# A planned one-core transformer loop: the causal mask moved from TensorE to VectorE, exponentials taken per head, gate columns carried by the value product, and the weight preparation moved into the loop

## What is computed

```python
# layer 0: self attention (causal), cross attention, feed-forward; 16 heads of 16
energy = where(cols >= length, -inf, Q @ K.T);  energy = where(cols > row, -inf, energy)   # causal: self only
z = softmax(energy / 4) @ V;  x1 = layernorm(x + z, ln1)
x2 = layernorm(x1 + mha(x1, ctx), ln2)
x3 = layernorm(x2 + relu(x2 @ fc1.T + b1) @ fc2.T + b2, ln3)
# layer 1 ("pair"): NX = layernorm(ctx, n1), NF = layernorm(x3, n2), one head of 256
h = gelu(softmax(NF @ NX.T / 16) @ NX @ gate.T + gate_b)      # 4 columns: the gates
cross = h @ w_cross.T + b;  NC = layernorm(cross, n3)
x4 = NF + gam2 * (cross + gam1 * softmax(NC @ NC.T / 16) @ NC)
# layer 2 ("real"): x5 = x4 + softmax(x4 @ ctx.T) @ ctx
# layer 3 ("mix"): 8 heads of 32; keys and values from layernorm(ctx, g1)
x6 = x5 + mha(layernorm(x5, g1), layernorm(ctx, g1));  U = (layernorm(x6, g2) @ W_in.T + b_in) @ Bmat
s = silu(s @ A.T) + U[t]                                       # a scan over the 128 rows
out = x6 + s @ Cmat + mean(program_probs) @ W_prog.T + b_prog
```

## Time and profile before

| | |
|---|---|
| median of 3 runs | 4208.76 us (4208.7 to 4211.23) |
| profiled execution, its time | 4207.95 us |
| its span | 4206.2 us |
| PE busy | 4042.6 us, 96% |
| weight loads of PE busy | 3383.5 us, 80% |
| DVE busy | 3431.2 us, 82% |
| ACT busy | 3175.7 us, 76% |
| POOL busy | 2911.0 us, 69% |

### The profile page before, as it was taken

The page is one execution under the profiler, slowest core; times in us unless marked ns, Lnnn a source line. Parts: engine busy times, 40 slices in busy tenths (PEclk is TensorE's granted clock), DMA queues, the critical chain, the costliest instruction groups (busy, mean ns, idle before and its releaser), DMA issues.

```text
span 4206.2 us, 112214 instructions
## 1 busy us (share of the span) xinstructions
PE 4042.6 (96%) x37547; PEld 3383.5 (80%) x37547; DVE 3431.2 (82%) x9517; ACT 3175.7 (76%) x6733; POOL 2911.0 (69%) x3172
## 2 busy tenths in 40 slices
PE   4899999999999999999999999999999999999859
PEld 3688888888888888888888888888888888888645
DVE  3688888888888888888888888888888888888634
ACT  1577887887788778877887787788778877887632
POOL 0477777777777777777777777777777777777634
PEclk9999999999999999999999999999999999999979
DMA  3000100010001100000100010101000000100037
GB/s 108 19 25 25 33 30 28 25 33 30 28 25 33 30 28 26 30 29 27 31 30 28 25 33 30 28 25 33 30 28 26 30 28 25 33 30 25 17 103 272
DMA packets 116547, 159.98 MB, mean 38 GB/s; under 512 B 11350, under 2 KB 103323, under 8 KB 111579
## 3 DMA queue, kind: packets, MB, share of 16 engines
q1 hardware_dynamic: 111626, 146.75, 11.2%
q10 hardware_dynamic: 4368, 6.17, 0.5%
HBM read 115.01 MB, written 37.88 MB: 36 GB/s over the span
## 4 chain that ended last, share of the span: by engine, by line
PE 67%; ACT 12%; POOL 7%; issue 5%; DVE 4%; DMA 0%; ACTq 0%; DVEq 0%; POOLq 0%; SPq 0%
PE bank L674 15%; PE bank L744 9%; PE bank L666 7%; PE bank L682 6%; PE bank L858 4%; PE bank L714 3%; ACT prob L992 3%; PE bank L778 3%; PE bank L693 3%; PE bank L773 2%; POOL rs_ln L1404 2%; PE bank L791 2%; POOL X L1424 2%; POOL X L1418 2%; ACT probT L1002 2%
## 5 line engine op out<-in xcount | busy, mean ns | idle before, releaser
L1158 DVE TENSOR_REDUCE mx<-bank 128x4 f32<-128x512 f32 x1280 | 837.6, 681 | 90.4 <-PE bank L714 68.6
L1169 DVE TENSOR_TENSOR prob<-bank,mx 128x512 f32<-128x512 f32 x1280 | 847.8, 679 | 54.6 <-PE bank L744 33.8
L1002 ACT ACTIVATE probT<-bank 128x512 f32<-128x512 f32 x1280 | 753.3, 600 | 158.9 <-PE bank L778 100.5
L992 ACT ACTIVATE prob<-prob 128x512 f32<-128x512 f32 x1280 | 795.6, 641 | 22.0 <-DVE prob L1169 20.9
L982 ACT ACTIVATE turned<-bank 128x512 f32<-128x512 f32 x896 | 531.9, 616 | 344.0 <-PE bank L666 223.5
L744 PE MATMUL bank<-ident,prob 128*128 128x128 f32 x5120 | 746.3, 277 | 20.3 <-DVE den L1180 6.5
L744 PEld LDWEIGHTS bank<-ident,prob 128*128 128x128 f32 x5120 | 591.3, 142 | 124.9 <-issue 36.8
L674 PE MATMUL bank<-turned,shared 128*128 128x256 f32 x2560 | 605.7, 384 | 1.8 <-ACT turned L982 1.8
L674 PEld LDWEIGHTS bank<-turned,shared 128*128 128x128 f32 x2560 | 468.3, 191 | 69.9 <-issue 14.3
L1404 POOL TENSOR_TENSOR rs_ln<-ve_ln,half 128x2 f32<-128x2 f32 x320 | 226.4, 707 | 384.9 <-DVE ve_ln L1147 384.9
L1483 POOL TENSOR_SCALAR shared<-turned,half_of 128x512 f32<-128x512 f32 x256 | 399.1, 1570 | 79.9 <-ACT turned L982 79.9
(11 more groups left out here) (242 smaller groups left out, 9047.8 us busy)
## 6 DMA issues: line engine op xcount, KB each, us to landing
shared<-in_x SPq DMA_DIRECT2D x128, 256.0 KB, 3.0
CB<-in_ctx SPq DMA_DIRECT2D x64, 256.0 KB, 3.4
CC<-in_ctx SPq DMA_DIRECT2D x64, 256.0 KB, 2.8
mod<-mod_rows SPq DMA_DIRECT2D x64, 256.0 KB, 3.3
residual<-X SPq DMA_DIRECT2D x64, 256.0 KB, 3.5
out<-turned SPq DMA_DIRECT2D x16, 1024.0 KB, 4.8
turned<-residual SPq DMA_DIRECT2D x14, 1024.0 KB, 7.3
u_turned<-us SPq DMA_DIRECT2D x64, 64.0 KB, 2.4
```

The lines of the kernel that those rows point to most:

```text
L992: nc.scalar.activation(flat(t), flat(t), ACT.Exp, scale=SCALE[p]).then_inc(*st["act"].mark(f"exp.{b}{r}"))
L1002: nc.scalar.activation(flat(t), banks.of(f"{att}.turn.{b}{r}")[:, :], ACT.Copy).then_inc(*st["act"].mark(f"probT.{b}{r}"))
L1158: nc.vector.tensor_reduce(m[:], banks.of(f"{att}.tile.{b}{r}")[:, :].rearrange("p (h t) -> p h t", h=4), AX, ALU.max)\
L1169: nc.vector.tensor_tensor(t[:], banks.of(f"{att}.tile.{b}{r}")[:, :].rearrange("p (h t) -> p h t", h=4), maxes.of(f"{att}.max.{b}{r}")[:]. ...
```

## The change

The self tiles lose `causal` on PE. DVE now adds the mask while it copies the bank into the `prob` buffer (`mask.br`), and takes the negated maximum out of that buffer (`max.br`); ACT takes the exponential in four instructions of 128 x 128, one a head, each with its head's negated maximum as bias; the scale 1/4 is folded into the query weights. The bank is free after `mask`, and the `prob` buffer is held from `mask` on.

The 4 gate columns ride on the value product of the mix layer (`w_v3`, 260 columns a batch, two banks, two `vp3` buffers). `vx`, its evacuation, `a4r`, `a4`, `yT` and its evacuation are gone. DVE divides the probabilities themselves (`part1`, two instructions of 128 x 128). `av1` has weights of 4 columns and moves 128, one batch in each of two strips, ACT takes the gelu of it with the bias column in two instructions of 4 x 128, and `cross` has weights of 32 rows, one batch in each strip and in a bank of its own, evacuated in two instructions. `mix_out.u` has weights of 64 columns, one batch in each half of the array.

The two blocks ahead of the loop are gone. Seven loads (identity, three weights of the first projections, three small ones) and the ordering of two weights stand ahead of it. The weights of the cross attention are loaded in turn 1, all others in turn 2 (54 DMAs in SP's queue), the probabilities in turn 2 from ACT's queue. The preparation (`prepare`) stands at the head of turn 3 on PE, ACT, DVE and POOL. The sum of the probabilities is now a tree of additions. `PROGRAM` and `BANKS` are written anew throughout; the number of turns is the same.

```diff
-                def causal_(b, r):
...
-                        nc.tensor.matmul(t[:, :], ident_b[:], causal[:].rearrange("p h t -> p (h t)"), start=True, stop=False,
-                                         skip_group_check=True).then_inc(*self_att["pe"].mark(f"causal.{b}{r}"))
...
-                                                    KEYS[p][rows_, a, :, b * S:(b + 1) * S], start=(p != "self"), stop=True,
-                                                    skip_group_check=(p == "self"))
+                                                    KEYS[p][rows_, a, :, b * S:(b + 1) * S], start=True, stop=True)
...
-                def vx(g):
...
+                def v3(g):
...
+                            last = nc.tensor.matmul(t[:, 0:D + 4], trn["HCT"][:, a, b * S:(b + 1) * S], w_v3[:, a, :],
+                                                    start=(a == 0), stop=(a == DH - 1))
...
-                        last = nc.tensor.matmul(t[:, b * 4:b * 4 + 4], pct["1"][:, b, :], vxs[:, b, :], start=True, stop=True)
+                        last = nc.tensor.matmul(t[32 * b:32 * b + 4, 0:S], vp3[g % 2][:, b, D:D + 4], pct["1"][:, b, :], start=True, stop=True)
...
-                def yT(g):
...
-                        last = nc.tensor.matmul(t[:, b * D:(b + 1) * D], y5T[:, b, :], w_cross[:], start=True, stop=True)
+                    for b, (t, _) in enumerate(took):
+                        rows_ = slice(32 * b, 32 * b + 32)
+                        last = nc.tensor.matmul(t[:, 0:D], y5T[rows_, :], w_cross[rows_, :], start=True, stop=True)
...
-                        last = nc.tensor.matmul(t[:, 0:W], w_u[:, a, :], trn["H6T"][:, a, :], start=(a == 0), stop=(a == DH - 1))
+                        for b in range(G):
+                            last = nc.tensor.matmul(t[NS * b:NS * b + NS, 0:S], w_u[:, a, :], trn["H6T"][:, a, b * S:(b + 1) * S],
+                                                    start=(a == 0), stop=(a == DH - 1))
...
+                def prepare():
...
+                    for w in latest(*(banks.free(n) for n in PREP_BANKS)):
+                        pe.wait_ge(*w)
+                    pe.wait_ge(rest_in, REST)
+                    pe.wait_ge(prep, 4)
+                    pe.wait_ge(ordered, 6)
...
+                    pe.wait_ge(prep, 8)
+                    pe.wait_ge(turned_b, 4)
+                    pe.wait_ge(means, 6)
...
+                    def masked(g):
...
+                        low = maxes.of(f"{att}.max.{b}{r}")
+                        for h in range(4):
+                            last = nc.scalar.activation(t[:, h, :], t[:, h, :], ACT.Exp, bias=low[:, h:h + 1], scale=1.0)
...
+                    def mask_(g):
+                        t, free = probs.claim(f"{att}.mask.{b}{r}", st["pe"], f"turn.{b}{r}")
...
+                        nc.vector.tensor_tensor(t[:], banks.of(f"{att}.tile.{b}{r}")[:, :].rearrange("p (h t) -> p h t", h=4),
+                                                causal[:].unsqueeze(1).to_broadcast([128, 4, 128]), ALU.add).then_inc(*st["dve"].mark(f"mask.{b}{r}"))
...
+                        nc.vector.tensor_reduce(m[:], probs.of(f"{att}.mask.{b}{r}")[:], AX, ALU.max, negate=True)\
...
+                def part1(g):
...
+                    for b in range(G):
+                        last = nc.vector.tensor_scalar(pc["1"][:, b, :], pc["1"][:, b, :], rsum["1"][:, b:b + 1], None, ALU.mult)
...
+def drive(eng, rings, handlers, engine, ahead=None):
...
+    for i in range(NG + LAGS):
+        if i in ahead:
+            ahead[i]()
         for unit, name, lag in ORDER[engine]:
```

712 lines of the change are left out of this document (354 added, 358 removed).

## The result

The changed kernel takes 4143.65 us (median of 4 runs, 4143.01 to 4149.18) beside 4208.73 for the kernel before in the same session: a ratio of 0.985, 95% interval 0.983 to 0.986. That is -65 us, where -227 was predicted; the time lies outside the range of 3900 to 4085. The profiled run took 4143.4 us.

What follows compares the result with a forecast made beforehand. TensorE's list was taken to bound the loop: its edits save 3.1 us a group, 62 x 3.1 = 192, and the start 35, so 4208 - 192 - 35 = 3981 us. Forecast 3945 to 4030 (0.50), wider range 3900 to 4085.

Steps and rivals of the forecast that it cites:

- What is taken from it shortens all 64 groups, as long as the others keep up.: Loop: TensorE's list, busy 60.5 of a 60.7 us turn, sets the turn, so cuts there shorten every group.
- 6.06 of 6.06 us: Profile reading of a loop stretch where ScalarE had nothing to spare; cited as a risk to hiding its added work.
- ScalarE's +4.2 us: Loop: four exponentials per self tile, 0.26 us each, for one of 0.52; +4.2 us a group, hidden on the average.
- Rivals 4 and 5: ScalarE half uncovered, 1.5 us a turn, 4074 us (0.06); slower, self exponentials' added time on the path, 4241 us (0.05).
- the sign I named: Forecast wrong if TensorE has over 1 us of new idle time a turn released by ScalarE's exponentials or evacuations.
- The narrow products: Loop, TensorE: `av1` -0.2, `cross` -0.4 and `u` -0.3 us a group from using narrow strips of the array.
- scores: Loop, TensorE: five bursts of three tiles and a lone tile cost +0.6 us a group, bounds +0.4 to +1.1.
- Rival 1: Narrow products gain nothing: -2.0 us a group, 4049 to 4085 us; changes of shape might add +0.8 a turn; chance 0.14.
- The bound of -3.9: Loop: largest saving a group on TensorE, with the bounds of its edits all on one side; the other end -1.7.
- VectorE no change, mask and maximum: Loop: mask addition and maximum out of the buffer cost VectorE the same for 8 tiles, within 0.05 us each.
- The start: Before the loop fills: first turn of x1 at 75 us in place of 110, -35 us, bounds -20 to -45.
- The end: Last turns and scan: number of turns, lags and scan taken as the same, so no change in time.

Runs made afterwards that it cites:

- e2: Changed kernel with ScalarE's two evacuations of `cross` moved ahead of the two `ln1` instructions; 4196.0 us.
- e5: Changed kernel with the gelu of the gates replaced by a copy with bias, so ScalarE loads no second table; 4090.4 us.
- e7: Changed kernel with TensorE reordered: two values products ahead of `cross`, two between it and the turn of the tile taking its bank; 4159.3 us.
- e3: Kernel before the change without its eight mask products a group, the causal mask left out; 4166.1 us.
- e1: Changed kernel with one exponential of 128x512 for each self tile, without the bias (maximum computed but not subtracted); 4146.5 us.
- e9: Changed kernel with the load of the modulation rows one turn earlier in SP's list, and the modulation stored one turn earlier; 4134.3 us.

## Why the prediction was wrong, point by point

- **"What is taken from it shortens all 64 groups, as long as the others keep up."** This is the step that failed: the overlap was taken for granted from averages. The sum of TensorE's edits was right (-2.9 for -3.1), and only 0.9 us of it reached the turn. I judged the others by busy time over a turn. What the runs show in its place is a stretch in which another engine works without a pause and TensorE hangs on its last instruction: 1.27 us of waits a turn in the passage (e2, e5, e7). The rows had a sign of it: 6.06 of 6.06 us, which I read as a threat to the exponentials alone. e3 shows that in the old order as well eight products of 1.93 us were worth 0.80. Of the 2.05 us between the edits' 2.93 and the turn's 0.88, new waits are 1.25 and changes of shape 0.28; about 0.5 is open.
- **ScalarE's +4.2 us is hidden.** Right, for the new order (e1: no gain from taking it back). Its size was too low: 0.29 us each, not 0.26, so 8 x (4 x 0.29 - 0.52) = +5.1 us. Rivals 4 and 5, exponentials on the path, did not happen; the sign I named, more than 1 us of new idle time "released by ScalarE's exponentials or evacuations", showed up in part: 0.50 us a turn is released by the gelu, 0.49 by the evacuation of `cross` and 0.28 by the exponential of a ctx tile, none by a self tile's.
- **The narrow products.** -0.64 for -0.9; `v` +0.13 for +0.03; scores +0.65 for +0.6. Small errors in size.
- **Rival 1's mechanism** (changes of shape, +0.8 us) came nearest in the number: "all other products" grew by 0.80 us. That agreement is luck in good part: I had priced a change at 0.2 us, where 0.093 is measured, so that four changes make 0.37 a turn, 0.28 of it in those products, and more than half of the 0.80 is something else. The rival's own -2.0 a group does not follow from its terms either: -1.73 - 0.81 + 0.03 - 0.33 + 1.06 is -1.8, and 4061 us.
- **The bound of -3.9** was mis-added: -2.84 - 0.31 - 0.44 - 0.43 + 0.4 is -3.6, so the low end of the range should have been 3918. The measured time lies far from it.
- **VectorE no change, mask and maximum.** Right: 512.4 us in 600, where 517.8 had been.
- **The start, -35.** Direction right, size off though inside its bounds of -20 to -45: the first turn of x at 8.3 us (11 forecast), the first turn of x1 at 87.8 (75), -22. All of SP's 54 issues, 0.48 us each and some up to 4, count before the preparation: the last load landed at 57 us. I had priced them by bytes. After them came 30 us of preparation, not 18 to 25; VectorE waits 4.6 us in it for the tree of sums, and TensorE 6.6. TensorE's clock is not the difference: it is granted 0.50 there, and the earlier trace rows has 1.00 for the preparation before, but the same four records took as long (before, then after):

```profile
49.89 2.05 PE L558 MATMUL bank<-w_v,CC 128*128 128x256 f32 x4
```
```profile
69.52 2.07 PE L806 MATMUL bank<-w_v,NC 128*128 128x256 f32 x4
```

- **The end, 0.** Wrong by 11.5 us. I wrote that lags and scan are the same, and did not read SP's row of the table, where one load changed its lag (e9).
- The turn accounts for most of the miss of 162 us: 3.1 x 62 = 192 forecast, 54 measured (49.6 in the 58 turns, 4.6 between the first turn of x1 and the first `u`), 138 short; the start is 13 short, and the end 11.5.

## What to carry to other kernels

In a loop whose order is written out for five engines, a TensorE that is busy all the time is not proof that its list is the only limit: look for the stretch where another engine runs without a pause up to the step that releases TensorE, and count what of the removed work lies there. A part that is costed by itself should be tried by itself in the old order before the sums are believed. A queue that only issues transfers is a list like the others: every entry that is moved past another needs its own line in the sum, at the start and at the end.
